# Asking for gathered edge tiles two at a time and announcing them two chunks later

## The chip, the cores and the metric

One core of a Trainium2 chip runs the whole program; the other cores are idle. The metric is the device time of one launch in microseconds, as a median over several launches. The engines are TensorE (PE), VectorE (DVE), ScalarE (ACT), GpSimd (POOL) and SyncE (SP); the last only starts transfers here, and POOL starts the indirect ones.

## The reference

50,000 nodes with 128 features, 50,000 edges sorted by target node. Two graph networks run one after the other. The first has three layers; `incidence[1]` is `dst`, so the messages are read at the targets and summed at `src`:

```python
for _ in range(DEPTH):                       # DEPTH = 3
    msgs = jnp.take(h, src, axis=0)
    msgs = jax.nn.relu(msgs @ W_edge + b_edge)
    agg = jax.ops.segment_sum(msgs, dst, num_segments=N_NODES)
    h = jax.nn.relu(jnp.concatenate([agg, h], axis=-1) @ W_agg + b_agg)
```

The second is a transformer layer on the same graph (queries, keys, values, edge features, a softmax over the edges of a node, a feed-forward part and layer norms). Both end in a residual sum and a layer norm.

## The kernel before, in words

The program is written by hand, stage by stage, with semaphores (`build`, line 1822):

- `sort_by_window` (line 193) sorts the edges by the 256-node block ("window", `W = 256`) in which their messages are summed, and makes the first messages. `window_tables` (line 535) computes tables from the sorted edges, among them `passed`: for each chunk of edge tiles, the number that the semaphore `tile_mm` must have reached once PE has used the chunk.
- `message_passing` (line 633) does the first two layers (`LAYERS - 1`), `last_layer` (line 925) the third one and the projections of the second network.
- `last_edges`, `attention` and `feed_forward` are the rest.

In the stages that the change touches, the messages of a layer lie in memory as rows of 3 x 128 bf16 numbers (`PARTS = 3`: high, middle and low part of a float). The sorted edges make 392 tiles of 128 edges (`NT`). For each tile POOL starts one indirect transfer, which gathers 128 rows of 768 bytes into one of 32 slots (`TILES`) of a ring in SBUF (`gathered`; line 759, in the last layer line 1076). PE multiplies each tile with a one-hot matrix made by DVE (`edge_hot`, line 856) and so sums the messages per node. It goes through 196 blocks of 256 nodes (`NW`), each with 3 tiles always (`ALWAYS`, of which neighbours share some), that is 9 matmuls on line 776, and rarely some more (`further`). After them come the product with the node's own row (line 794), and of the blocks before it the products for the next messages (lines 799 and 805). ACT and DVE close the block (lines 824 to 837, 874, 879), and SP stores it.

What POOL and PE tell each other:

- `g_in`: the transfers of a tile count up by 16 when they have landed.
- `tile_in`: POOL waits for `g_in` of a group of tiles and then adds their number (`tell`, lines 743 to 745 and 1060 to 1062). PE waits on it before a block: `pe.wait_ge(tile_in, layer * NT + first + ALWAYS)` (line 788).
- `tile_mm`: PE counts the blocks and extra tiles that it has added. Before POOL overwrites the slots of a chunk, it waits until `tile_mm` has reached the number in `passed` (lines 751 to 756). Those numbers are loaded to registers four at a time (lines 753 and 1070).

Before the change a chunk has 8 tiles (`CHUNK`), and tiles are announced in groups of 4 (`TOLD`). Within a chunk POOL issues eight gathers. The first group of the chunk is announced ahead of the eighth gather, the second group at the head of the next chunk, directly behind the gathers that it waits for:

```python
for c in range(NT // CHUNK):
    old = c - TILES // CHUNK
    if c:
        tell(c * CHUNK // TOLD - 1)      # waits for the 4 gathers issued last
```

All instructions of POOL are in one queue, in the order written.

Of the kernel before, what the change touches and what calls it, by code (L numbers as in the profile page):

```python
# [24 lines left out]
NT = NG * T  # L25
# [4 lines left out]
NW = NP // W  # L30
RING = 4
MSGS = 8
PARTS = 3
TILES = 32
CHUNK = 8
TOLD = 4
ALWAYS = 3
HOTS = 4
LAST = (N - (NG - 1) * GR) // T
# [1 line left out]
FAR = 65536  # L41
BIG = 3.0e38
EPS = 1e-5
assert NW % RING == 0 and NT % CHUNK == 0 and TILES % CHUNK == 0 and CHUNK % TOLD == 0
assert NG % 2 == 0 and (N - (NG - 1) * GR) % T == 0 and N == E


# [49 lines left out]
class Core:  # L97


    def __init__(self, nc, ctx):  # L100
# [23 lines left out]
        self.more_before = ctx.enter_context(nc.sbuf_tensor("more_before", [1, NW], I32))  # L124
        self.passed = ctx.enter_context(nc.sbuf_tensor("passed", [1, NT // CHUNK + 3], I32))
        self.column = ctx.enter_context(nc.sbuf_tensor("column", [P, 520], F32))
# [408 lines left out]
def window_tables(core):  # L535

    nc = core.nc
    with ExitStack() as s:
        def sb(nm, shape, dt):
            return s.enter_context(nc.sbuf_tensor("wt_" + nm, shape, dt))  # L540
        pair_i = sb("pair_i", [P, T, P, 2], I32)
        col_f, dst_f = sb("col_f", [P, T, P], F32), sb("dst_f", [P, T, P], F32)
        first_i, first_f, again, again_all = sb("first_i", [1, NT], I32), sb("first_f", [1, NT], F32), sb("again", [1, NT], F32), sb("again_all", [1, NT], F32)
        passed_f = sb("passed_f", [1, NT // CHUNK - 1], F32)
        filled, loaded, float_ok, transposed, tabs, chain = (core.sem("wt_" + x) for x in (
# [9 lines left out]
        def _(dve):  # L555
# [18 lines left out]
            dve.wait_ge(chain, 6)  # L574
            last = NT // CHUNK - 1
            chunks = [x[:, :].rearrange("a (c k) -> a c k", k=CHUNK) for x in (first_f, again_all)]
            nc.vector.scalar_tensor_tensor(out=passed_f[:, :], in0=chunks[0][:, 1:last + 1, 0], scalar=2.0, in1=chunks[1][:, 0:last, CHUNK - 1],
                                           op0=ALU.add, op1=ALU.add).then_inc(chain, 1)
# [54 lines left out]
def message_passing(core, W_edge, b_edge, W_agg, b_agg):  # L633
# [3 lines left out]
    with ExitStack() as s:  # L637
# [13 lines left out]
        wts, tabs_ok = core.sem("mp_weights_in"), core.sem("mp_place_tables")  # L651
        h_ld, h_st = ([core.sem(f"mp_{n}{r}") for r in range(RING)] for n in ("h_loaded", "h_stored"))
        m_st, m_uses = [core.sem(f"mp_m_stored{r}") for r in range(MSGS)], [(NW - r + MSGS - 1) // MSGS for r in range(MSGS)]
        g_in = [core.sem(f"mp_gathered{r}") for r in range(TILES // TOLD)]
        tile_in, edge_hot_ok, win_mm = core.sem("mp_tile_in"), core.sem("mp_edge_hots"), core.sem("mp_block_summed")
        more_hot_ok, tile_mm = ([core.sem(f"mp_{n}{layer}") for layer in range(LAYERS - 1)] for n in ("more_hots", "tiles_added"))
        h_ok, u_mm, u_ok, m_mm = core.sem("mp_h_ready"), core.sem("mp_u_product"), core.sem("mp_u_ready"), core.sem("mp_m_product")
# [35 lines left out]
        with nc.Block() as block:  # L693
# [41 lines left out]

            @block.gpsimd
            def _(pool):
                told = [0] * (TILES // TOLD)
                for layer in range(LAYERS - 1):
                    if layer:  # L740
                        for r in range(MSGS):
                            pool.wait_ge(m_st[r], 16 * layer * m_uses[r])
                    def tell(quarter):
                        pool.wait_ge(g_in[quarter % (TILES // TOLD)], 16 * TOLD * told[quarter % (TILES // TOLD)])
                        pool.sem_inc(tile_in, TOLD)

                    for c in range(NT // CHUNK):
                        old = c - TILES // CHUNK
                        if c:
                            tell(c * CHUNK // TOLD - 1)  # L750
                        if old >= 0:
                            if old % 4 == 0:
                                passed = nc.values_load_multi_w_load_instructions(
                                    core.passed[0:1, bass.ds(old, 4)], engines=[pool.engine], min_val=1, max_val=NW + NT + 1)[1]
                            pool.wait_ge(tile_mm[layer], passed[old % 4])
                            pool.nop(nofuse=True)
                        for i in range(c * CHUNK, (c + 1) * CHUNK):
                            r, q = i % TILES, i // TOLD % (TILES // TOLD)
                            pool.indirect_dma_start(gathered[:, r * PARTS * D:(r + 1) * PARTS * D], None, core.msg_rows[layer % 2],  # L759
                                                    bass.IndirectOffsetOnAxis(ap=core.other_idx[:, i:i + 1], axis=0)).then_inc(g_in[q], 16)  # L760
                            if i % TOLD == TOLD - 1:
                                if i % CHUNK >= TOLD:
                                    tell(i // TOLD - 1)
                                told[q] += 1
                    tell(NT // TOLD - 1)

            @block.tensor
            def _(pe):
# [156 lines left out]
def last_layer(core, W_agg, b_agg, x, w, b):  # L925
# [6 lines left out]
    with ExitStack() as s:  # L932
# [20 lines left out]
        wts, parts_c, zero_ok, tabs_ok = (core.sem("ll_" + n) for n in ("weights_in", "parts_chain", "zeros_ready", "place_tables"))  # L953
        h_ld, x_ld = [core.sem(f"ll_h_loaded{r}") for r in range(RING)], [core.sem(f"ll_x_loaded{q}") for q in range(Q)]
        st_x1, st = ([core.sem(f"ll_{n}{k}") for k in range(2)] for n in ("x1_stored", "proj_stored"))
        g_in = [core.sem(f"ll_gathered{r}") for r in range(TILES // TOLD)]
        tile_in, edge_hot_ok, block_mm, more_hot_ok, tile_mm = (core.sem("ll_" + n) for n in (
            "tile_in", "edge_hots", "block_summed", "more_hots", "tiles_added"))
        dst_hot_ok, dst_mm = core.sem("ll_dst_hots"), core.sem("ll_dst_counted")
# [95 lines left out]

        @block.gpsimd
        def _(pool):
            told = [0] * (TILES // TOLD)

            def tell(quarter):  # L1060
                pool.wait_ge(g_in[quarter % (TILES // TOLD)], 16 * TOLD * told[quarter % (TILES // TOLD)])
                pool.sem_inc(tile_in, TOLD)

            for c in range(NT // CHUNK):
                old = c - TILES // CHUNK
                if c:
                    tell(c * CHUNK // TOLD - 1)
                if old >= 0:
                    if old % 4 == 0:
                        passed = nc.values_load_multi_w_load_instructions(  # L1070
                            core.passed[0:1, bass.ds(old, 4)], engines=[pool.engine], min_val=1, max_val=NW + NT + 1)[1]
                    pool.wait_ge(tile_mm, passed[old % 4])
                    pool.nop(nofuse=True)
                for i in range(c * CHUNK, (c + 1) * CHUNK):
                    r, q = i % TILES, i // TOLD % (TILES // TOLD)
                    pool.indirect_dma_start(gathered[:, r * PARTS * D:(r + 1) * PARTS * D], None, core.msg_rows[(LAYERS - 1) % 2],  # L1076
                                            bass.IndirectOffsetOnAxis(ap=core.other_idx[:, i:i + 1], axis=0)).then_inc(g_in[q], 16)
                    if i % TOLD == TOLD - 1:
                        if i % CHUNK >= TOLD:
                            tell(i // TOLD - 1)  # L1080
                        told[q] += 1
            tell(NT // TOLD - 1)

        @block.tensor
        def _(pe):
# [736 lines left out]
def build(nc, a, out):  # L1822
    with ExitStack() as ctx:
        core = Core(nc, ctx)
        l1 = {name[7:]: ap for name, ap in a.items() if name.startswith("L1_gnn_")}
        make_identity(core)
        core.end_stage()
        sort_by_window(core, a["dst"], a["src"], a["x"], a["L0_gnn_W_edge"], a["L0_gnn_b_edge"], a["L0_gnn_W_agg"])
        core.end_stage()

        window_tables(core)
        core.end_stage()
        message_passing(core, a["L0_gnn_W_edge"], a["L0_gnn_b_edge"], a["L0_gnn_W_agg"], a["L0_gnn_b_agg"])
        core.end_stage()
        last_layer(core, a["L0_gnn_W_agg"], a["L0_gnn_b_agg"], a["x"], l1, l1)
        core.end_stage()
        last_edges(core)
        core.end_stage()
        attention(core, a["edge_attr_64"], l1["We"])
        core.end_stage()  # L1840
        feed_forward(core, l1, out)
# [16 lines left out]
```

## Time and profile before

| what | value |
|---|---|
| median of 3 launches | 5096.5 us (5095.79 to 5099.93) |
| profiled execution, span from first to last instruction | 6166.6 us |
| profiled execution, mean granted TensorE clock | 0.792 of full speed |
| busy over the span: PE, DVE, ACT, POOL | 74%, 59%, 34%, 51% |
| `sort_by_window` and `window_tables` | 0 to 857 us |
| `message_passing`, two layers | 858 to 2576 us |
| `last_layer` | 2576 to 3800 us |
| attention, then feed-forward | to 5150 us, to 6166 us |

The profiled execution's own time is its span: nothing else is printed for it. It is 1070 us longer than the median of the launches without a profile, and all durations below come from the profiled one. In the profile's rows PE's matmuls are pipelined, so their durations overlap; "issue" is idle time for which no releaser is seen.

### The profile page before, as it was taken

Reading aid. Unit: us, or ns where it says so; the run is one execution under the profiler, and the core shown is the slowest. Engines: PE = TensorE matmul, PEld = TensorE weight load, DVE = VectorE, ACT = ScalarE, POOL = GpSimd, SP = SyncE. Lnnn points to the kernel's source line nnn. Section 1 sums busy time; section 2 is a strip of 40 time slices with the busy share of each in tenths; the row PEclk is TensorE's granted clock in tenths of the full one; section 3 lists DMA queues with packets and bytes.
Section 4 is the critical chain, followed back from the end, with each engine's and each line's share of the span. In section 5 each row is a group of like instructions: output and inputs, shape, how many; then the busy total and the mean of one; then the engine's idle time right before and its main releaser. Section 6 shows DMA issues by size and latency. Waiting matters only on the chain. (4 is left out here: it accounts for less than half of the span.)

```text
span 6166.6 us, 106939 instructions
## 1 busy us (share of the span) xinstructions
PE 4568.4 (74%) x21995; PEld 2882.5 (47%) x21996; DVE 3657.1 (59%) x12075; ACT 2092.9 (34%) x4610; POOL 3168.2 (51%) x3348
## 2 busy tenths in 40 slices
PE   5666657777767777688888887566666666888887
PEld 3444435555555555555555554344444443333333
DVE  7666643333333333466666655677777776777777
ACT  0222223333333333322323323222222223666665
POOL 1555554444344444333333332666666664888887
PEclk9888878888888888889999998555555556999999
DMA  0333335555545555455665655333333332333333
GB/s 26 128 129 127 124 123 150 149 151 152 152 146 151 149 151 149 144 172 174 187 189 174 187 176 156 86 90 88 92 90 88 90 88 69 107 103 106 104 103 96
DMA packets 690049, 789.03 MB, mean 128 GB/s; under 512 B 145529, under 2 KB 545648, under 8 KB 689900
## 3 DMA queue, kind: packets, MB, share of 16 engines
q1 hardware_dynamic: 577004, 568.56, 28.9%
q0 software_dynamic: 112896, 218.94, 14.0%
q14 instruction: 112, 0.92, 0.1%
q8 instruction: 37, 0.61, 0.0%
HBM read 414.24 MB, written 372.92 MB: 128 GB/s over the span
## 5 line engine op out<-in xcount | busy, mean ns | idle before, releaser
L759 POOL DMA_INDIRECT mp_gathered<-msg_rows,other_idx x784 | 746.7, 952 | 947.8 <-PE bank L776 626.1
L776 PE MATMUL bank<-mp_edge_hot,mp_gathered 128*128 128x256 bf16 x3528 | 606.6, 304 | 279.3 <-issue 227.7
L1076 POOL DMA_INDIRECT ll_gathered<-msg_rows,other_idx x392 | 386.7, 987 | 782.8 <-PE bank L1096 607.7
L525 POOL DMA_INDIRECT by_window<-so_pay,so_pos_i x392 | 395.0, 1008 | 438.1 <-issue 303.9
L1363 POOL DMA_INDIRECT at_kv<-kv_rows,kv_idx x392 | 426.8, 1089 | 343.0 <-DVE at_v_e L1512 236.7
L776 PEld LDWEIGHTS bank<-mp_edge_hot,mp_gathered 128*128 x3528 | 373.4, 106 | 452.1 <-issue 383.9
L879 DVE TENSOR_TENSOR mp_msg_out<-mp_rest,mp_msg_out 128x256 bf16<-128x256 f32 x392 | 166.6, 425 | 649.1 <-ACT mp_msg_out L837 379.7
L1647 POOL DMA_INDIRECT ff_agg<-at_rows,last_idx x392 | 414.1, 1056 | 97.2 <-issue 89.7
L1365 POOL DMA_INDIRECT at_q<-q_rows,node_idx x392 | 390.0, 995 | 123.4 <-issue 123.4
L1143 PE MATMUL bank<-ll_weights,ll_x_cols 128*128 128x512 f32 x784 | 424.1, 643 | 4.5 <-issue 4.4
L824 ACT ACTIVATE mp_h_out<-bank,mp_b_agg 128x256 f32<-128x256 f32 x392 | 186.1, 475 | 702.3 <-PE bank L794 400.8
L1761 PE MATMUL bank<-ff_gelu,ff_w 128*128 128x512 f32 x784 | 412.9, 630 | 1.1 <-ACT ff_gelu L1793 1.1
L1753 PE MATMUL bank<-ff_h_cols,ff_w 128*128 128x512 f32 x784 | 386.7, 617 | 2.4 <-issue 2.4
L856 DVE TENSOR_SCALAR mp_edge_hot<-digits,mp_first_col,column 128x256 bf16<-128x256 bf16 x1176 | 336.9, 348 | 77.7 <-issue 48.9
L1096 PE MATMUL bank<-ll_gathered,ll_edge_hot 128*128 x3528 | 270.8, 226 | 141.4 <-issue 136.2
L794 PE MATMUL bank<-mp_h_in,mp_w_agg_h 128*128 128x256 f32 x784 | 305.0, 476 | 68.0 <-issue 65.2
L1424 PE MATMUL bank<-at_we,at_attr_cols 64*128 64x128 f32 x784 | 199.4, 431 | 193.2 <-ACT at_attr_cols L1458 100.3
L874 DVE TENSOR_TENSOR mp_rest<-bank,mp_msg_out 128x256 f32<-128x256 f32 x392 | 164.8, 420 | 294.8 <-issue 172.9
L406 DVE CUSTOM_DVE_ANT_0 so_picked<-so_onehot,bank 128x256 f32<-128x256 bf16 x392 | 164.4, 419 | 270.7 <-remote 158.8
L905 POOL TENSOR_TENSOR ff_rstd<-ff_eps_var,ff_half 128x4 f32<-128x4 f32 x294 | 307.1, 1045 | 24.5
L805 PEld LDWEIGHTS bank<-mp_w_agg_a,mp_msg_cols 128*128 128x128 f32 x1568 | 282.2, 228 | 77.2 <-issue 45.6
L805 PE MATMUL bank<-mp_w_agg_a,mp_msg_cols 128*128 128x128 f32 x1568 | 287.7, 314 | 29.1 <-issue 28.0
(247 smaller groups left out, 10008.7 us busy)
## 6 DMA issues: line engine op xcount, KB each, us to landing
msg_rows<-mp_msg_out SPq DMA_DIRECT2D x392, 192.0 KB
mp_h_in<-h_cols SPq DMA_DIRECT2D x392, 128.0 KB
h_cols<-mp_h_out SPq DMA_DIRECT2D x392, 128.0 KB
kv_rows<-ll_proj SPq DMA_DIRECT2D x98, 512.0 KB
msg_rows<-so_msg_out SPq DMA_DIRECT2D x98, 384.0 KB
h_cols<-so_h_out SPq DMA_DIRECT2D x98, 256.0 KB
ll_h_in<-h_cols SPq DMA_DIRECT2D x196, 128.0 KB
x_rows<-ll_x_b SPq DMA_DIRECT2D x98, 256.0 KB
```

The costliest lines, as they stand in the source:

```text
L525: pool.indirect_dma_start(core.by_window, bass.IndirectOffsetOnAxis(ap=pos_i[k][:, t:t + 1], axis=0), pay[k][:, t, :], None, bounds_check= ...
L759: pool.indirect_dma_start(gathered[:, r * PARTS * D:(r + 1) * PARTS * D], None, core.msg_rows[layer % 2], bass.IndirectOffsetOnAxis(ap=cor ...
L776: product = nc.tensor.matmul(agg_bank[k], gathered[:, bass.ds(at + d * D, D)], hot, start=(first and d == 0), stop=True, skip_group_check= ...
L805: product = nc.tensor.matmul(msg_bank[r % 2][:, c * P:(c + 1) * P], msg_c[r % 2][:, c * P:(c + 1) * P], w_agg_a[:, :], start=True, stop=True)
L856: return nc.vector.tensor_scalar(to, core.digits[:, :], first_col[:, bass.ds(n, 1)], core.column[:, bass.ds(i, 1)], ALU.add, ALU.is_equal)
L1076: pool.indirect_dma_start(gathered[:, r * PARTS * D:(r + 1) * PARTS * D], None, core.msg_rows[(LAYERS - 1) % 2], bass.IndirectOffsetOnAxis ...
L1143: nc.tensor.matmul(proj_bank[t][:, :], x1_cols[q % 2][:, t * P:(t + 1) * P], weights[:, :], start=t < T - BY_ACT, stop=True, skip_group_ch ...
L1363: pool.indirect_dma_start(kv[g % DEEP][:, t, :], None, core.kv_rows, bass.IndirectOffsetOnAxis(ap=core.kv_idx[:, at:at + 1], axis=0)).then ...
L1365: pool.indirect_dma_start(q[g % DEEP][:, t, :], None, core.q_rows, bass.IndirectOffsetOnAxis(ap=core.node_idx[:, at:at + 1], axis=0)).then ...
L1647: pool.indirect_dma_start(agg[g % 2][:, t, :], None, core.at_rows, bass.IndirectOffsetOnAxis(ap=core.last_idx[:, at:at + 1], axis=0)).then ...
L1753: nc.tensor.matmul(hid_bank[c][:, :], w1[:, c * P:(c + 1) * P], h_c[k][:, :], start=True, stop=True).then_inc(f1, 1)
L1761: product = nc.tensor.matmul(out_bank[k][:, :], w2[:, c, :], act_c[c][:, :], start=(c == 0), stop=(c == FC - 1))
```

## The change

`CHUNK` goes from 8 to 2. `TOLD` is gone: a chunk is also the group that is announced. It is announced after the gathers of the chunk two further on (`BEHIND = 2`), no longer directly behind its own. The wait for `tile_mm` and the two instructions around it come once for every 2 tiles, and the table `passed` has four times as many entries. There are 16 semaphores `g_in` in place of 8. The two stages are changed alike.

```diff
-CHUNK = 8
-TOLD = 4
+CHUNK = 2
+BEHIND = 2
@@ message_passing
-        g_in = [core.sem(f"mp_gathered{r}") for r in range(TILES // TOLD)]
+        g_in = [core.sem(f"mp_gathered{r}") for r in range(TILES // CHUNK)]
@@ pool
-                told = [0] * (TILES // TOLD)
                 for layer in range(LAYERS - 1):
+                    before = layer * NT // CHUNK
...
-                    def tell(quarter):
-                        pool.wait_ge(g_in[quarter % (TILES // TOLD)], 16 * TOLD * told[quarter % (TILES // TOLD)])
-                        pool.sem_inc(tile_in, TOLD)
+                    def tell(c):
+                        r = (before + c) % (TILES // CHUNK)
+                        pool.wait_ge(g_in[r], 16 * CHUNK * ((before + c) // (TILES // CHUNK) + 1))
+                        pool.sem_inc(tile_in, CHUNK)
 
                     for c in range(NT // CHUNK):
                         old = c - TILES // CHUNK
-                        if c:
-                            tell(c * CHUNK // TOLD - 1)
                         if old >= 0:
                             if old % 4 == 0:
                                 passed = nc.values_load_multi_w_load_instructions(
...
                         for i in range(c * CHUNK, (c + 1) * CHUNK):
-                            r, q = i % TILES, i // TOLD % (TILES // TOLD)
+                            r, q = i % TILES, (before + c) % (TILES // CHUNK)
                             pool.indirect_dma_start(gathered[:, r * PARTS * D:(r + 1) * PARTS * D], None, core.msg_rows[layer % 2],
                                                     bass.IndirectOffsetOnAxis(ap=core.other_idx[:, i:i + 1], axis=0)).then_inc(g_in[q], 16)
-                            if i % TOLD == TOLD - 1:
-                                if i % CHUNK >= TOLD:
-                                    tell(i // TOLD - 1)
-                                told[q] += 1
-                    tell(NT // TOLD - 1)
+                        if c >= BEHIND:
+                            tell(c - BEHIND)
+                    for c in range(NT // CHUNK - BEHIND, NT // CHUNK):
+                        tell(c)
```

POOL's queue in `message_passing` around the first time that slots are used again. "waits" lists the semaphores on which the instruction, or a bare wait just ahead of it, waits; where a semaphore number served an earlier stage, it stands here with that stage's name (the names with `so_` are those of `g_in`, and `so_ranks_ready` is `tile_mm`). Before:

```order
L759 DMA mp_gathered<-msg_rows,other_idx 128x384 [waits so_tables,so_flags]
L759 DMA mp_gathered<-msg_rows,other_idx 128x384 x7
L753 TENSOR_LOAD passed [waits so_flags_stored,so_onehots]
L753 ISA x8
L759 DMA mp_gathered<-msg_rows,other_idx 128x384 [waits so_ranks_ready]
L759 DMA mp_gathered<-msg_rows,other_idx 128x384 x7
L759 DMA mp_gathered<-msg_rows,other_idx 128x384 [waits so_bits,so_columns,so_ranks_ready]
L759 DMA mp_gathered<-msg_rows,other_idx 128x384 x7
```

After (here `mp_tiles_added0` is `tile_mm`):

```order
L753 TENSOR_LOAD passed [waits so_ranks_ready]
L753 ISA x8
L759 DMA mp_gathered<-msg_rows,other_idx 128x384 [waits mp_tiles_added0]
L759 DMA mp_gathered<-msg_rows,other_idx 128x384
L759 DMA mp_gathered<-msg_rows,other_idx 128x384 [waits so_ranks_read,mp_tiles_added0]
L759 DMA mp_gathered<-msg_rows,other_idx 128x384
L759 DMA mp_gathered<-msg_rows,other_idx 128x384 [waits so_positions,mp_tiles_added0]
L759 DMA mp_gathered<-msg_rows,other_idx 128x384
L759 DMA mp_gathered<-msg_rows,other_idx 128x384 [waits so_bits,mp_tiles_added0]
L759 DMA mp_gathered<-msg_rows,other_idx 128x384
L753 TENSOR_LOAD passed [waits so_columns]
L753 ISA x8
```

The waits for landings and for PE move from every eighth gather to every second one, and a load of four table entries with its eight register instructions comes before every eighth gather, not before every thirty-second. PE's queue has the same instructions as before.

## Rows read from the trace of the kernel before

**Rows 1.** The page's first line.

```profile
span 6166.6 us, 106939 instructions
```

**Rows 2.** Stretches: PE, PEld, DVE, ACT, POOL busy (instructions); granted clock; DMA share; GB/s

```profile
858.00:1712.00 854.00, 637.48 (x3359) 472.80 (x3359) 307.36 (x988) 297.47 (x783) 373.20 (x392) 0.83 0.50 150
1712.00:2576.00 864.00, 633.00 (x3359) 473.54 (x3359) 312.98 (x991) 299.12 (x785) 373.51 (x392) 0.82 0.50 150
2576.00:3800.00 1224.00, 1032.15 (x6621) 649.99 (x6621) 777.79 (x3066) 355.58 (x785) 386.71 (x392) 0.91 0.59 179
```

**Rows 3.** Waits of PE, 858 to 2576 us: total us, times, longest.

```profile
PE bank L776 <- issue: 263.0, 335, 4.4
PE bank L776 <- POOLq L745: 52.1, 13, 14.0
```

**Rows 4.** Waits of POOL, same stretch.

```profile
POOL mp_gathered L759 <- PE bank L776: 626.1, 85, 10.0
POOL mp_gathered L759 <- DMA mp_gathered<-msg_rows,other_idx: 26.6, 18, 3.2
```

**Rows 5.** PE's register instructions on L776: ns min/median/max, first and last start.

```profile
L776 PEldq FUSED_REGOPS  x3600: 2/46/1399, 866.0 to 2567.9; - x190
```

**Rows 6.** PE's timeline (start, us): two starts of a block, then a stall within a block.

```profile
1309.46 1.15 PE L776 MATMUL bank<-mp_edge_hot,mp_gathered 128*128 128x256 bf16 x9
...
1311.76 1.15 PE L776 MATMUL bank<-mp_edge_hot,mp_gathered 128*128 128x256 bf16 x9
...
1317.75 0.41 PE L776 MATMUL bank<-mp_edge_hot,mp_gathered 128*128 128x256 bf16 x2 [1.28 <-issue]
```

**Rows 7.** PE's timeline: two starts of a block at half clock.

```profile
1670.38 2.13 PE L776 MATMUL bank<-mp_edge_hot,mp_gathered 128*128 128x256 bf16 x9
...
1674.86 1.22 PE L776 MATMUL bank<-mp_edge_hot,mp_gathered 128*128 128x256 bf16 x9
```

**Rows 8.** POOL's timeline (start, us): seventh and eighth gather of the first chunk, later chunk heads.

```profile
865.85 0.95 POOL L759 DMA_INDIRECT mp_gathered<-msg_rows,other_idx  x1 [0.30 <-issue]
867.10 0.95 POOL L759 DMA_INDIRECT mp_gathered<-msg_rows,other_idx  x1 [0.30 <-issue]
870.57 0.95 POOL L759 DMA_INDIRECT mp_gathered<-msg_rows,other_idx  x1 [2.52 <-DMA mp_gathered<-msg_rows,other_idx]
...
882.84 0.95 POOL L759 DMA_INDIRECT mp_gathered<-msg_rows,other_idx  x1 [2.57 <-DMA mp_gathered<-msg_rows,other_idx]
...
895.56 0.95 POOL L759 DMA_INDIRECT mp_gathered<-msg_rows,other_idx  x1 [2.99 <-DMA mp_gathered<-msg_rows,other_idx]
...
909.49 1.01 POOL L759 DMA_INDIRECT mp_gathered<-msg_rows,other_idx  x1 [4.14 <-PE bank L776]
```

**Rows 9.** POOL's queue: the load of L753, the wait instruction of L756.

```profile
L753 POOLq TENSOR_LOAD <-passed x24: 322/326/545, 907.2 to 2512.6; - x24
...
L756 POOLq EVENT_SEMAPHORE  x90: 17/17/17, 908.7 to 2519.9; - x90
```

**Rows 10.** Instructions that mark the groups of the sort, last layer and attention.

```profile
L525 POOL DMA_INDIRECT by_window<-so_pay,so_pos_i x392: 969/974/1245, 128.1 to 834.9; - x196
...
L1143 PE MATMUL bank<-ll_weights,ll_x_cols x784: 589/592/1221, 2648.6 to 3796.8; 128*128 128x512 f32 x196
...
L1363 POOL DMA_INDIRECT at_kv<-kv_rows,kv_idx x392: 943/949/1860, 3812.9 to 5093.8; - x196
```

**Rows 11.** Timelines of POOL and ACT: two group starts each, sort, last layer, attention.

```profile
141.74 1.09 POOL L525 DMA_INDIRECT by_window<-so_pay,so_pos_i  x1 [3.45 <-issue]
...
147.00 1.10 POOL L525 DMA_INDIRECT by_window<-so_pay,so_pos_i  x1 [0.33 <-issue]
...
2773.96 0.60 ACT L1173 ACTIVATE ll_x_cols<-bank 128x512 f32<-128x512 f32 x1 [7.93 <-PE bank L1132]
...
2783.36 0.60 ACT L1173 ACTIVATE ll_x_cols<-bank 128x512 f32<-128x512 f32 x1 [2.92 <-PE bank L1132]
...
4314.32 0.95 POOL L1363 DMA_INDIRECT at_kv<-kv_rows,kv_idx  x1 [4.36 <-DVE at_v_e L1512]
...
4325.43 0.95 POOL L1363 DMA_INDIRECT at_kv<-kv_rows,kv_idx  x1 [0.30 <-issue]
```

**Rows 12.** Waits of POOL in the last layer, 2576 to 3800 us.

```profile
POOL ll_gathered L1076 <- PE bank L1096: 607.7, 43, 20.6
```

More of the change, by code:

```diff
@@ L43 @@
 EPS = 1e-5
-assert NW % RING == 0 and NT % CHUNK == 0 and TILES % CHUNK == 0 and CHUNK % TOLD == 0
+assert NW % RING == 0 and NT % CHUNK == 0 and TILES % CHUNK == 0 and ALWAYS + BEHIND * CHUNK < TILES - 2 * CHUNK
 assert NG % 2 == 0 and (N - (NG - 1) * GR) % T == 0 and N == E
@@ L955, in last_layer @@
         st_x1, st = ([core.sem(f"ll_{n}{k}") for k in range(2)] for n in ("x1_stored", "proj_stored"))
-        g_in = [core.sem(f"ll_gathered{r}") for r in range(TILES // TOLD)]
+        g_in = [core.sem(f"ll_gathered{r}") for r in range(TILES // CHUNK)]
         tile_in, edge_hot_ok, block_mm, more_hot_ok, tile_mm = (core.sem("ll_" + n) for n in (
@@ L1057, in _, with tell @@
         def _(pool):
[L1058 to L1062, printed above, removed]
+            def tell(c):
+                pool.wait_ge(g_in[c % (TILES // CHUNK)], 16 * CHUNK * (c // (TILES // CHUNK) + 1))
+                pool.sem_inc(tile_in, CHUNK)
             for c in range(NT // CHUNK):
                 old = c - TILES // CHUNK
-                if c:
-                    tell(c * CHUNK // TOLD - 1)
                 if old >= 0:
@@ L1074, in _ @@
                 for i in range(c * CHUNK, (c + 1) * CHUNK):
-                    r, q = i % TILES, i // TOLD % (TILES // TOLD)
+                    r, q = i % TILES, c % (TILES // CHUNK)
                     pool.indirect_dma_start(gathered[:, r * PARTS * D:(r + 1) * PARTS * D], None, core.msg_rows[(LAYERS - 1) % 2],
                                             bass.IndirectOffsetOnAxis(ap=core.other_idx[:, i:i + 1], axis=0)).then_inc(g_in[q], 16)
[L1078 to L1082, printed above, removed]
+                if c >= BEHIND:
+                    tell(c - BEHIND)
+            for c in range(NT // CHUNK - BEHIND, NT // CHUNK):
+                tell(c)
         @block.tensor
```

## Prediction

> **What bounds the kernel now.** I read the stretches first, then each engine's waits, then timelines. The two layers of message passing take 854 and 864 us of the profiled span [rows 2]. PE looks like the bound there: POOL spends 626.1 us waiting for PE to free slots, PE only 52.1 us waiting for POOL to announce tiles [rows 3, 4]. Taken at its word this says that nothing POOL does matters. But the span is 6166.6 us [rows 1] against a median of 5096.5 us without the profiler, and PE's idle time is mostly "issue", 263.0 us on the edge matmuls alone [rows 3]. It falls between matmuls of one block, where no semaphore is waited for [rows 6]. There even register instructions of PE, which touch nothing outside their queue, take 46 ns at the median and up to 1399 [rows 5]. I read that as PE's queue held up by the recording of its own many instructions, which is absent in a launch that is timed. POOL has few instructions, and its gathers come at a steady beat. So each engine must be priced without the stalls.
>
> PE: undisturbed, a block starts every 1311.76 - 1309.46 = 2.30 us [rows 6]; at half clock every 1674.86 - 1670.38 = 4.48 us [rows 7]. Two layers have 392 blocks: 902 us at full clock.
>
> POOL: two gathers are 1.25 us apart within a chunk (867.10 - 865.85). Where POOL does not wait for PE, the next chunk's first gather starts 3.47 us after the eighth (870.57 - 867.10), because the announcement waits for the gather just issued to land. The chunk heads are 12.27 and 12.72 us apart (882.84 - 870.57, 895.56 - 882.84) [rows 8]. I take 7 x 1.25 + 3.5 = 12.25 us for 8 tiles. Two layers have 98 chunks: 1201 us, and 24 loads of table entries in the same queue. The first load starts at 907.2, the wait instruction behind it at 908.7, with 545 ns in the load itself; at the median of 326 ns that is 1.3 us [rows 9]. 24 x 1.3 = 31, so POOL needs **1232 us** where PE needs 902. Without recording, POOL's queue bounds this stage: 3.14 us per block.
>
> A ledger checks this. The 1070 us between profile and median must come from stages with stalls. Sort: groups run from 128.1 to 834.9 us, 707 us for 98, while an undisturbed one takes 5.26 us, so 515: 192 us gone. Last layer: 1148 us from first to last projection against 98 x 9.40 = 921: 227. Attention: 1281 against 98 x 11.11 = 1089: 192 [rows 10, 11]. That leaves 1070 - 611 = 459 us for message passing: 1718 - 459 = 1259 us. POOL's bound with some 25 us at the layers' heads and ends gives 1257. With PE the bound at full clock it would be about 930, and the ledger would be 330 us off. The ledger is rough (one group stands for 98), but it sides with POOL.
>
> **The change part by part.**
> *Landing waits gone.* An announcement now waits for tiles whose last gather started 4 gathers, 5.0 us, earlier, and they have landed by then: the 3.47 us of the boundary hold landing and the start of the next gather both. Each boundary of eight gives up 3.5 - 1.25 = 2.25 us. There are 96 in two layers (the announcement that ends a layer stays): **-216 us**. Bounds: 2.2 (870.57) to 2.7 us (895.56) [rows 8], so -211 to -259.
> The boundary is also priced by a rule. The Trainium skill ("DMA: Bandwidth & Descriptors", Anatomy of one DMA) gives a transfer from GpSimd 2.0 us plus bytes over 436e3; for 98,304 bytes an estimate of 2.23 us. With the 0.8 us to the next gather the boundary would be 3.0 us, not 3.47, and the whole sum 48 us smaller in gain. The trace decides, for 3.47.
>
> *Waits every second gather.* Per pair POOL now issues one announcement and one wait for `tile_mm`, 17 ns each [rows 9]. Once a wait is over, a gather starts 909.49 - 908.7 = 0.8 us later [rows 8, 9]. An announcement already stands ahead of every eighth gather, and that gather still starts 1.25 us after the seventh with 0.30 us idle [rows 8]: the queue runs ahead, beneath the 0.95 us of the gather that executes. With 0.3 us until the queue is free, 0.1 for two instructions and 0.8 for the start there are 1.2 of 1.25 us used. I take **0**. Lower bound 0, since nothing is removed here. Upper bound 0.6 us per pair: the wait holds until the gather ahead is done, 0.95 + 0.1 + 0.8 = 1.85 in place of 1.25, so 0.6; times 392 pairs that is 235 us. I lean to the low end since the row of the eighth gather is this very case.
>
> *Loads.* 180 chunks of a layer wait for slots, with a load for every fourth: 45, before 12. Two layers: 90 for 24. A load in a running burst costs 0.3 + 0.1 + 1.3 + 0.8 - 1.25 = 1.2 us: 90 x 1.2 = 108, less the 31 of before: **+77 us**. Bounds: 0.7 us each if part of it is hidden (+32), 1.5 with the longest load seen (+104).
>
> *First announcement.* PE's first block needs 3 tiles. Before, tiles 0 to 3 are announced ahead of the eighth gather; now tiles 2 and 3 behind it: 1.3 us later in each of three layers. It costs only where PE then sets the pace, **+2 us** with the last layer's.
>
> *Last layer.* POOL waits 607.7 us for PE there [rows 12] of 1224, and needs 49 x 12.25 = 600 us where an undisturbed stage takes 921. Its queue stays hidden; with 343 fewer waits it could be faster without anyone seeing it. The cover is PE's and DVE's work of 9.40 us per group against POOL's 6.1. **0 us.** The longer `passed` table costs DVE a fraction of a microsecond.
>
> Sum: -216 + 77 + 2 = -137 us. POOL's queue falls to 784 x 1.25 + 108 = 1088 us, 2.78 us per block, still above PE's 2.30, so PE's full-clock pace does not cut the gain. The sum is made on differences in the profiled execution's durations and applied to the median, as the recording stalls that separate the two are on PE and not in these terms: 5096.5 - 137 = **4960 us**.
>
> **The rivals.**
> *A. PE bounds the stage in timed launches too.* Granted clock in message passing is 0.82 to 0.83 [rows 2]; at 4.48 us a block for part of the time PE could average 3.1 to 3.3 us, and the ledger's 1259 us (3.2 per block) fits that as well. The waits of rows 3 and 4 then tell the truth. Against it: the clock is lower where PE is less busy (0.83 with PE busy 75% of the stretch, 0.91 with 84% [rows 2]), and without stalls and without waits for POOL nothing would leave PE idle to keep it down. Then the change moves POOL's slack alone: 5096.5 + 2, range 5080 to 5100. A mixture (PE the bound in half of the time) gives about 5028 and belongs to my range.
> *B. The wait breaks POOL's run-ahead.* Asking before every second gather ties POOL to each gather's end: 235 us more, and loads as before. -216 + 77 + 235 = +96: about 5193 if POOL is the bound. It decides from (216 - 77) / 392 = 0.35 us per pair; below that the change still gains. For it: only 0.05 us of slack in my count. Against it: the eighth gather.
> *C. The transfers become the bound.* DMA share is 0.50 at 150 GB/s [rows 2]; squeezed to 1120 us it would be 0.77. Landing times then grow; up to 5.0 us they stay hidden. If half of the gain is lost so, 5028.
>
> **How the numbers follow.** Forecast with its sizes somewhat off: 0.65. A: 0.16. B: 0.12, of which a third is too mild to be slower than noise. C or the mixture: 0.07. Low end: -259 + 32 = -227, little of it likely together: 4890. The high end takes in C and most of A's neighbourhood: 5092. Changes within 0.2% (10 us, about what a measurement of this kernel can tell from none) are same. Faster 0.74: forecast, C, and a part of A and B. Same 0.15: most of A. Slower 0.11.
>
> **What would show it.** In the changed profile POOL's waits on its own landings (26.6 us in 18 pieces [rows 4]) are gone; where POOL runs free, pairs follow each other at 1.25 us, with one 2.4 us step every 8 gathers; at 1.8 us or more per pair head B holds. In the profile itself the stage shrinks little, since PE's stalls remain: 1718 us to between 1640 and 1720, and POOL's long waits for PE turn into many short ones. If the time is within 10 us of before, A is right and my reading of the stalls is wrong.

## The result and the profile after

The changed kernel takes **4900.4 us** (median of 4, 4899.9 to 4902.8) against 5097.4 us before (median of 4, 5095.8 to 5099.9): a ratio of 0.9616, 95% interval 0.9604 to 0.9627, 197 us or 3.8% faster. The forecast was 4960, range 4890 to 5092.

```profile
span 4898.1 us, 108529 instructions
```

This span is within 2 us of the execution's own time, and it records as many instructions of PE as before. In some periods a chip runs the kernel before in 5974 to 6199 us: by its span and stalls the first profile [rows 1, 5] falls in one, and so do the runs with BEHIND = 0, BEHIND = 1 and chunks of 4, each compared with the kernel before run beside it.

The kernel before was profiled again (the run "before again"). Its page begins, and PE's register instructions on L776 read:

```profile
span 5081.5 us, 106939 instructions
...
L776 PEldq FUSED_REGOPS  x3600: 46/46/65, 679.4 to 1978.0; - x190
```

As many instructions are recorded as in [rows 1] and [rows 5], and the longest of these takes 65 ns, not 1399. So the 1070 us between the first profile and the median are not the price of recording.

The stretches that answer to [rows 2], of before again (first layer, second, last; columns as there):

```profile
672.00:1329.00 657.00, 555.48 (x3359) 436.71 (x3359) 308.77 (x997) 291.23 (x784) 375.77 (x392) 0.92 0.65 197
1329.00:1989.00 660.00, 554.90 (x3359) 433.61 (x3359) 305.42 (x985) 290.74 (x784) 376.19 (x393) 0.93 0.64 195
1989.00:2959.00 970.00, 923.55 (x6627) 576.69 (x6627) 780.28 (x3076) 356.05 (x785) 386.67 (x395) 0.98 0.75 226
```

and of the changed kernel:

```profile
672.00:1233.00 561.00, 510.26 (x3359) 413.54 (x3359) 306.60 (x998) 288.49 (x784) 376.75 (x393) 0.98 0.77 231
1233.00:1799.00 566.00, 515.82 (x3359) 416.83 (x3359) 302.77 (x981) 288.83 (x784) 376.75 (x392) 0.97 0.76 227
1799.00:2768.00 969.00, 921.85 (x6627) 575.48 (x6627) 781.68 (x3079) 355.94 (x785) 375.09 (x395) 0.98 0.73 227
```

Message passing falls from 1317 to 1127 us. The last layer takes 970 and 969 us: nothing. PE is busy 84% of the stretch before and 91% after, and its granted clock goes from 0.92 and 0.93 to 0.98 and 0.97. The transfers' share goes from 0.65 to 0.77.

The waits of POOL and PE that answer to [rows 3, 4], of before again from 670 to 1990 us:

```profile
POOL mp_gathered L759 <- DMA mp_gathered<-msg_rows,other_idx: 168.9, 82, 3.7
POOL mp_gathered L759 <- PE bank L776: 83.3, 23, 5.5
POOL ll_gathered L1076 <- POOLq L144: 20.9, 1, 20.9
POOL mp_gathered L759 <- DMA msg_rows<-mp_msg_out: 19.2, 1, 19.2
...
PE bank L776 <- POOLq L745: 150.1, 66, 13.4
```

and of the changed kernel, from 670 to 1800 us:

```profile
POOL ll_gathered L1071 <- POOLq L144: 51.4, 1, 51.4
POOL mp_gathered L759 <- DMA msg_rows<-mp_msg_out: 49.9, 1, 49.9
POOL mp_gathered L759 <- PE bank L775: 42.8, 58, 3.2
...
POOL mp_gathered L759 <- DMA mp_gathered<-msg_rows,other_idx: 20.1, 66, 0.3
...
PE bank L775 <- POOLq L747: 52.2, 26, 14.3
```

Here, without PE's stalls, POOL waited for its own landings, 169 us, where [rows 4] had 27, and PE waited for POOL. That is what the prediction inferred for a launch without stalls. After the change the landing waits are gone (no piece is longer than 0.3 us, the gap that stands between any two gathers), and the two waits between a layer's last gather and the next one's first (20.9 and 19.2 us) have grown to 51.4 and 49.9: PE now ends a layer later than POOL.

POOL's timeline of before again (start, duration): the eighth gather of a chunk and the head of the next, once where a load of table entries stands between and once without.

```profile
718.22 0.98 POOL L759 DMA_INDIRECT mp_gathered<-msg_rows,other_idx  x1 [0.30 <-issue]
724.53 0.95 POOL L759 DMA_INDIRECT mp_gathered<-msg_rows,other_idx  x1 [5.33 <-issue]
...
733.35 0.95 POOL L759 DMA_INDIRECT mp_gathered<-msg_rows,other_idx  x1 [0.30 <-issue]
736.83 0.94 POOL L759 DMA_INDIRECT mp_gathered<-msg_rows,other_idx  x1 [2.54 <-DMA mp_gathered<-msg_rows,other_idx]
```

The head without a load comes 3.48 us after the gather before it, as in [rows 8]; the one with a load 6.31. Over both layers the 72 heads without a load average 3.70 us, the 24 with one 5.42. Together that is 396 us, where 96 steps of 1.25 would be 120: 276 us of POOL's queue.

The same timeline of the changed kernel, over a stretch in which a load is executed:

```profile
762.29 0.99 POOL L759 DMA_INDIRECT mp_gathered<-msg_rows,other_idx  x1 [0.30 <-PE bank L775]
763.59 0.95 POOL L759 DMA_INDIRECT mp_gathered<-msg_rows,other_idx  x1 [0.30 <-issue]
764.84 0.95 POOL L759 DMA_INDIRECT mp_gathered<-msg_rows,other_idx  x1 [0.30 <-PE bank L775]
766.09 1.00 POOL L759 DMA_INDIRECT mp_gathered<-msg_rows,other_idx  x1 [0.30 <-issue]
767.39 0.94 POOL L759 DMA_INDIRECT mp_gathered<-msg_rows,other_idx  x1 [0.30 <-issue]
```

Every gather follows the one before at 1.25 to 1.30 us; the load starts at 763.1. The trace holds 90 loads:

```profile
L753 POOLq TENSOR_LOAD <-passed x90: 322/341/1145, 711.9 to 1734.5; - x90
```

The 90 gathers behind a load start 1.44 us after the one before on average, 74 of them less than 1.6 us, so all loads together cost the queue at most 17 us.

The ledger from first gathers: layer one's gathers 636.8 to 509.5 us, layer two's 637.5 to 514.2, so 251 us less; the turn of POOL to layer two 20.2 to 50.9 and to the last layer 21.9 to 52.4 us, 61 us given back. 251 - 61 = 190 us. The two spans differ by 183, as the rest of the program came out some 6 us longer in this pair. In the run with the change in message passing alone, on the same chip as before again, the span is 191 us shorter, 190 of them in this stage.

What paces PE now is seen in its timeline in the changed kernel: ordinary blocks, and one in which it loads the table of the next eight blocks.

```profile
1001.88 0.70 PE L793 MATMUL bank<-mp_h_in,mp_w_agg_h 128*128 128x256 f32 x2
...
1004.44 0.69 PE L793 MATMUL bank<-mp_h_in,mp_w_agg_h 128*128 128x256 f32 x2
...
1006.92 0.70 PE L793 MATMUL bank<-mp_h_in,mp_w_agg_h 128*128 128x256 f32 x2
```

```profile
942.81 0.70 PE L793 MATMUL bank<-mp_h_in,mp_w_agg_h 128*128 128x256 f32 x2
...
945.17 1.70 PE L775 MATMUL bank<-mp_edge_hot,mp_gathered 128*128 128x256 bf16 x9 [0.78 <-DVE mp_edge_hot L855]
947.07 0.69 PE L793 MATMUL bank<-mp_h_in,mp_w_agg_h 128*128 128x256 f32 x2 [0.21 <-issue]
```

```profile
L680 PEldq TENSOR_LOAD <-spans x50: 592/776/1262, 675.7 to 1778.3; - x50
...
L680 PEldq TENSOR_LOAD <-spans x1: 1040/1040/1040, 943.5 to 943.5; - x1
```

Ordinary blocks are 2.56 and 2.48 us apart, the one with the load (line 680) 4.26. The second row is the load of that block: it holds PE's queue until 944.5, just before the late edge matmuls, so the 0.78 us that the view puts down to DVE are the load's. The mean over a layer is 2.78 and 2.81 us, of which 0.13 at most are waits for POOL (52 us in all): PE, not POOL at 2.50, sets the pace.

### The profile page after: what moved, and what is told of

It is laid out like the page before. It is cut to its first block and busy times, and to the rows that moved or that the text cites. A ratio compares the mean times of both kernels' runs of the same rounds, so it can differ in the third digit from the quotient of the medians.

```text
span 4898.1 us, 108529 instructions
## 1 busy us (share of the span) xinstructions
PE 4105.9 (84%) x21995; PEld 2654.1 (54%) x21996; DVE 3644.4 (74%) x12075; ACT 2076.8 (42%) x4610; POOL 3180.5 (65%) x3348
## 5 line engine op out<-in xcount | busy, mean ns | idle before, releaser
L775 PE MATMUL bank<-mp_edge_hot,mp_gathered 128*128 128x256 bf16 x3528 | 476.5, 275 | 61.8 <-POOLq L747 34.9
L1359 POOL DMA_INDIRECT at_q<-q_rows,node_idx x392 | 410.6, 1047 | 119.4 <-issue 119.4
L775 PEld LDWEIGHTS bank<-mp_edge_hot,mp_gathered 128*128 x3528 | 346.5, 98 | 133.8 <-issue 91.0
L1137 PE MATMUL bank<-ll_weights,ll_x_cols 128*128 128x512 f32 x784 | 405.1, 619 | 0.0
L1793 ACT ACTIVATE ff_xhat<-ff_y,ff_shift,ff_rstd 128x128 f32<-128x128 f32 x392 | 161.6, 482 | 333.9 <-DVE ff_shift L1669 332.1
L793 PE MATMUL bank<-mp_h_in,mp_w_agg_h 128*128 128x256 f32 x784 | 275.0, 433 | 11.0 <-issue 9.0
L1787 ACT ACTIVATE ff_gelu<-bank,ff_bf 128x512 f32<-128x512 f32 x392 | 245.4, 675 | 58.1 <-PE bank L1747 58.1
L1747 PEld LDWEIGHTS bank<-ff_h_cols,ff_w 128*128 128x128 f32 x784 | 154.4, 197 | 199.2 <-issue 171.9
L804 PEld LDWEIGHTS bank<-mp_w_agg_a,mp_msg_cols 128*128 128x128 f32 x1568 | 238.3, 192 | 21.9 <-ACT mp_msg_cols L827 1.2
L1707 DVE SCALAR_TENSOR_TENSOR ff_v<-ff_deviation,ff_rstd,ff_x 128x128 f32<-128x128 f32 x392 | 114.6, 352 | 173.6 <-POOL ff_rstd L904 171.8
```

The source lines that it names most:

```text
L775: product = nc.tensor.matmul(agg_bank[k], gathered[:, bass.ds(at + d * D, D)], hot, start=(first and d == 0), stop=True, skip_group_check= ...
L1137: nc.tensor.matmul(proj_bank[t][:, :], x1_cols[q % 2][:, t * P:(t + 1) * P], weights[:, :], start=t < T - BY_ACT, stop=True, skip_group_ch ...
L1359: pool.indirect_dma_start(q[g % DEEP][:, t, :], None, core.q_rows, bass.IndirectOffsetOnAxis(ap=core.node_idx[:, at:at + 1], axis=0)).then ...
L1747: nc.tensor.matmul(hid_bank[c][:, :], w1[:, c * P:(c + 1) * P], h_c[k][:, :], start=True, stop=True).then_inc(f1, 1)
```

## The experiments

**Before again** (no edit).

> The kernel before, unchanged, for a second profile. Theory 1 (the first profile of the kernel before was of an execution that was itself 1070 us longer, and its PE stalls are no part of a normal one): span within 10 us of 5097, no gaps of over 1 us between the nine edge matmuls of a block, message passing 1258 to 1330 us with chunk heads of POOL 12.2 to 12.7 us apart and POOL waiting for PE under 60 us. Rival (PE bounds message passing in every launch): span near 5097 too, but POOL waits for PE over 150 us in message passing. It also tells how long the last layer takes: the changed kernel has it at 978 us; under theory 1 within 10 us of that, under theory 2 (the finer asking helped the last layer) 1020 to 1050 us.

Span 5081.5 us, time 5083.3. Theory 1 holds in its main points: stage 1317 us, PE's waits for POOL 150 us. Chunk heads without a load are 12.2 to 13.7 us apart, 12.5 at the median, so some exceed the 12.7 expected. POOL's waits for PE, 83 us, lie between the two theories' numbers. The last layer takes 970 us, so theory 2 falls.

**Half of the change each.** In the first, the last layer keeps chunks of 8 and a second table for them; in the second, message passing does.

```diff
+CHUNK8 = 8
+TOLD = 4
...
-for c in range(NT // CHUNK):
+for c in range(NT // CHUNK8):      # shortened: in one stage only
```

> Message passing as changed, the last layer with chunks of 8 and announcements of 4. Theory 1 (all of the gain is in message passing): 4900, within 10 us of the changed kernel. Theory 2 (the last layer gave what the prediction missed, 60 us): 4950 to 4965, and the last layer's stretch longer by that.

> The last layer as changed, message passing with chunks of 8 and announcements of 4. Theory 1: 5097, within 10 us. Theory 2: 5035 to 5050. The sum of this run's gain and that of the other half should be 197 us if the two stages are independent.

Message passing alone: 4894.4 us against 5085.4, ratio 0.9626 (0.9610 to 0.9642). Last layer alone: 5085.1, ratio 0.9998 (0.9989 to 1.0008). All of the gain is in message passing; the last layer's cover held, as forecast.

**Landing wait alone.** Chunks stay at 8; the second announcement of a chunk moves behind the fourth gather of the next one.

```diff
-                        if c:
-                            tell(c * CHUNK // TOLD - 1)
...
-                                if i % CHUNK >= TOLD:
+                                if i >= TOLD:
                                     tell(i // TOLD - 1)
```

> The kernel before with one thing changed in both stages: the second group of 4 of a chunk is announced behind the fourth gather of the next chunk, not at its head. Chunks stay at 8, table loads as before. It takes away the landing wait alone. Theory 1 (landing wait is what is paid): message passing shrinks by 96 x 2.25 = 216 us less the waits for PE that come back; 4890 to 4930 in all if the last layer does not matter. Theory 3 (the coarse asking costs too, since 8 slots are asked for at once and the ring runs full): only 90 to 150 us gained, 4950 to 5005, and POOL waits for PE in pieces of some us at the chunk heads.

4899.5 us against 5085.4, ratio 0.9631 (0.9615 to 0.9647): all but 5 us of what message passing alone gives on the same chip (4894.4), with one announcement moved. Its stretches of message passing, beside 561 and 566 us of the changed kernel:

```profile
673.00:1236.00 563.00, 513.43 (x3359) 416.98 (x3359) 306.35 (x998) 289.31 (x784) 379.50 (x393) 0.98 0.76 230
1236.00:1805.00 569.00, 515.45 (x3359) 415.72 (x3359) 300.73 (x982) 288.99 (x784) 378.93 (x392) 0.98 0.74 226
```

So the chunk size has a part of 5 us at most in this result. Theory 3 falls.

**Four times the loads.** The changed kernel, with a load of four entries, each from the entry that the pair needs, ahead of every pair.

```diff
-                            if old % 4 == 0:
+                            if True:
...
-                            pool.wait_ge(tile_mm[layer], passed[old % 4])
+                            pool.wait_ge(tile_mm[layer], passed[0])
```

> The changed kernel with a load of four table entries ahead of every second gather, not of every eighth: 270 loads more in message passing. Theory 1 (POOL's queue runs ahead of the gathers that execute, so a load costs nothing while it fits beneath two gathers, 2.5 us): within 15 us of the changed kernel. The prediction's price (1.2 us each, exposed): 320 us more in message passing alone. Between (the queue needs 0.3 to 0.5 us beyond two gathers for each pair): 100 to 200 us more, less what PE's slower pace hides.

4980.5 us against 5098.0, ratio 0.9770 (0.9754 to 0.9786). That is 80 us slower than the changed kernel, below the 100 to 200 of the nearer of the two dear prices. POOL's timeline, then the loads ahead of the third and of the fifth of these gathers, and all of them:

```profile
902.99 0.99 POOL L759 DMA_INDIRECT mp_gathered<-msg_rows,other_idx  x1 [1.02 <-PE bank L775]
904.28 1.04 POOL L759 DMA_INDIRECT mp_gathered<-msg_rows,other_idx  x1 [0.30 <-issue]
906.00 0.95 POOL L759 DMA_INDIRECT mp_gathered<-msg_rows,other_idx  x1 [0.68 <-issue]
907.26 0.95 POOL L759 DMA_INDIRECT mp_gathered<-msg_rows,other_idx  x1 [0.31 <-issue]
908.51 0.94 POOL L759 DMA_INDIRECT mp_gathered<-msg_rows,other_idx  x1 [0.30 <-PE bank L775]
...
L753 POOLq TENSOR_LOAD <-passed x1: 953/953/953, 903.3 to 903.3; - x1
...
L753 POOLq TENSOR_LOAD <-passed x1: 326/326/326, 906.4 to 906.4; - x1
...
L753 POOLq TENSOR_LOAD <-passed x360: 321/956/2054, 708.8 to 1859.4; - x180
```

A pair starts 3.01 us (906.00 - 902.99) after the last where its load takes 953 ns, and 2.51 us where it takes 326. So this edit changed two things, the number of the loads and their length. The 90 loads that start at an entry whose number is a multiple of four, as all loads of the changed kernel do, take 0.36 us on average, and the gather behind them starts 1.31 us after the one before. The other 270 take 1.11 us, and the step is 1.91. Why the first entry matters the runs don't show. The layers' gathers grow by 82 and 69 us, and the turns at their ends shrink back from 51 and 52 to 18 and 20, so 85 us in the stage. The cost is that of the long loads: a short one is hidden even directly behind a pair whose load was long. Short loads ahead of every pair were not run.

**Load ahead of the landing wait.** The kernel before, with the load of the next entries moved above the announcement at the chunk head.

```diff
+                        if old >= 0 and old % 4 == 0:
+                            passed = nc.values_load_multi_w_load_instructions(
+                                core.passed[0:1, bass.ds(old, 4)], engines=[pool.engine], min_val=1, max_val=NW + NT + 1)[1]
                         if c:
                             tell(c * CHUNK // TOLD - 1)
                         if old >= 0:
-                            if old % 4 == 0:
-                                passed = nc.values_load_multi_w_load_instructions(
...
```

> The kernel before, with the load of table entries put ahead of the announcement at the chunk head, so that it runs while the landing is waited for. In the second profile of the kernel before, chunk heads without a load are 3.4 to 3.6 us behind the gather before, those with one 5.3 to 6.1. If that difference is the load standing behind the landing wait: 24 x 1.3 to 2.1 = 30 to 50 us less, 5035 to 5055. If it is something else that comes every fourth chunk (PE's wait for slots): within 10 us of before.

5071.1 us against 5098.0, ratio 0.9945 (0.9929 to 0.9962): 27 us, just below the range. The heads with a load average 4.10 us, down from 5.42 in before again, so the load did stand behind the landing wait, at 1.3 us each: 24 x 1.3 = 31. But the 72 heads without one rise from 3.70 to 3.96, 19 us, so some 12 us are left in the stage. The kernel before was not profiled on this chip, and where the other 15 us of the 27 lie stays open.

**Less work for PE.** In both kernels `add_tile` of message passing leaves out the third part of each message (the low parts are missing from the sums).

```diff
-                        for d in range(PARTS):
+                        for d in range(PARTS - 1):
```

> The changed kernel; in message passing PE adds two of the three parts of each message, 6 edge matmuls per block instead of 9, so the low parts are missing from the sums. Theory 4 (after the change PE bounds message passing: its lag behind POOL grows to the full ring and takes 30 us more at each layer's end): its stage falls by 60 to 100 us to POOL's 1.25 us per gather, 4800 to 4840. Rival (POOL is the bound after the change as the prediction said): within 15 us of 4900.

> The kernel before with the same matmuls left out. Theory 1 (POOL's queue bounds message passing before the change): 5097 less at most 20 us (the 83 us that POOL waits for PE in 23 pieces can give back a part), so 5060 to 5097. Rival A of the prediction (PE is the bound before the change too): 5000 or less.

The changed kernel: 4820.1 us, 80 us below its 4900. Its stretches and the turns at the layers' ends:

```profile
673.00:1202.00 529.00, 457.56 (x2762) 359.41 (x2762) 306.74 (x999) 289.15 (x784) 380.14 (x393) 0.98 0.81 245
1202.00:1726.00 524.00, 455.02 (x2762) 360.44 (x2762) 302.48 (x983) 289.25 (x784) 376.37 (x393) 0.97 0.81 245
```

```profile
POOL ll_gathered L1071 <- POOLq L144: 20.2, 1, 20.2
```

The kernel before: 5086.2 us against 5098.0, ratio 0.9976 (0.9967 to 0.9986), 12 us. The same cut in PE's work is worth 80 us after the change and 12 before. POOL bounded the stage before; PE bounds it after. Rival A and the prediction's own statement that PE would not cut the gain both fall. So does rival C: the stage got shorter with the transfers' share at 0.81 and 245 GB/s, above the 0.77 of the changed kernel.

**No distance between gather and announcement.** `BEHIND = 0`, otherwise as changed; the kernel before took 5998 us beside it.

> The changed kernel with BEHIND = 0: each pair of tiles is announced directly behind its own gathers. This puts a landing wait behind every second gather, four times as many as before the change. Theory 1 (a landing wait costs POOL 2.2 us and POOL then bounds): a pair takes 1.25 + 3.5 = 4.75 us, message passing 392 x 4.75 = 1862 us plus 90 loads of 1.3 to 2.1: 5700 to 5850 in all, the last layer (196 x 4.75 = 931 plus loads, against PE's 920) longer by 20 to 120 us as well. If small chunks were good in themselves, less than 5400.

6419.5 us in one run, against 5998.1: 421 us slower, where the changed kernel is faster. POOL's timeline shows the wait behind each pair:

```profile
1002.07 0.96 POOL L759 DMA_INDIRECT mp_gathered<-msg_rows,other_idx  x1 [0.31 <-issue]
1007.02 0.95 POOL L759 DMA_INDIRECT mp_gathered<-msg_rows,other_idx  x1 [3.99 <-PE bank L775]
1008.27 0.94 POOL L759 DMA_INDIRECT mp_gathered<-msg_rows,other_idx  x1 [0.30 <-issue]
1012.26 0.99 POOL L759 DMA_INDIRECT mp_gathered<-msg_rows,other_idx  x1 [3.04 <-DMA mp_gathered<-msg_rows,other_idx]
```

The heads come 4.95 and 3.99 us after the gather before, 1.5 and 0.5 more than the 3.5 expected. The absolute time can't be compared with the expectation, which was written for a kernel before of 5097 us; direction and place are as expected. Small chunks are worth nothing without the distance.

**Distance of one chunk, with chunks of 2 and of 4.**

```diff
-CHUNK = 2
-BEHIND = 2
+CHUNK = 2        # in the other run: 4
+BEHIND = 1
```

> The changed kernel with BEHIND = 1: an announcement waits for tiles whose last gather started two gathers (2.5 us) earlier. Landings take 2.7 us from the start of the gather. Theory 1: the queue is held up to 2.7 us and loses its run-ahead: each pair 2.7 + 0.1 + 0.8 = 3.6 us after the last gather it waits for, which is 2 x 1.25 = 2.5 plus 1.1, so a pace of about 3.6 us per pair at worst; message passing up to 1400 us, 5000 to 5180 in all. If the queue's start time of 0.8 us is hidden all the same: within 40 us of the changed kernel.

> The changed kernel with chunks of 4 and BEHIND = 1: an announcement waits for tiles whose last gather started four gathers (5.0 us) earlier, as in the changed kernel, with half of its waits, announcements and loads. Theory 1 (only the age of the landing that is waited for counts): within 10 us of the changed kernel. If the number of waits costs something: 10 to 60 us less than the changed kernel.

> The kernel with BEHIND = 1 again, since its first run fell on a chip where the kernel before takes 5998 us, not 5097, and the changed kernel has no time there. On a chip where the kernel before takes 5080 to 5100: if the landing waited for is too young (2.7 us from the start of the gather against 2.5 us until the next start), 5000 or more; if POOL's start time is hidden beneath the gather that executes and PE's pace bounds all the same, 4895 to 4925. On a slow chip: near 5483, a ratio near 0.915.

All three fell where the kernel before takes 5998 or 6181 us. Chunks of 2: 5482.7 us against 5998.1, ratio 0.9148 (0.9118 to 0.9179), and again 5662.2 against 6181.3, ratio 0.9151 (0.9122 to 0.9180), the ratio expected for such a chip, though not the time. Chunks of 4: 5549.0, ratio 0.9236 (0.9201 to 0.9271). The gain is larger there, 8.5% with chunks of 2, and chunks of 4 lose 66 us to chunks of 2, though the landings they wait for are older; nothing here explains either. The numbers expected beside 5080 to 5100 us were not tested, and the changed kernel itself has no time beside these.

The stalls of [rows 5] are there too. In the second of these runs, chunks of 2 again:

```profile
L775 PEldq FUSED_REGOPS  x3600: 2/46/737, 865.7 to 2289.3; - x190
```

## Why the prediction was right in direction and short in size

- **What bounds.** Right: without PE's stalls POOL's queue bounds message passing, at 3.3 us per block against 3.14 worked out. The run with less work for PE before the change gives 12 us and shows it. Wrong: the cause of the stalls. I read them as the price of recording; before again records as many instructions of the same kernel without them, and the changed kernel's trace as many of PE's. What held PE's queue up in the first profile stays open. It was luck that the forecast came to no harm by this: the launches of the result had no such stalls, but not for the reason given.
- **The ledger** gave the stage 1259 us, POOL's pace 1257; it takes 1317. The undisturbed groups of the sort and attention were good (first to last gather of the sort 520 us against 515); the last layer took 970 us, not the 921 plus 75 of heads and ends that its group and stretch gave, so the ledger was off by stages as well.
- **Landing waits, -216 us.** Right in mechanism, undersized: the heads without a load average 3.70 us, not 3.5, so 96 x (3.70 - 1.25) = 235. By the Trainium skill's figure ("DMA: Bandwidth & Descriptors", Anatomy of one DMA), from which the prediction worked out an estimate of 3.0 us for the boundary, the term would have been further off.
- **Waits every second gather, 0.** Right in number; rival B did not happen. Heads of pairs without a load start 1.31 us after the gather before, and 1.26 in the run with less work for PE. But the evidence was misread, and in so far it was luck. No announcement stands ahead of the eighth gather, other than the section on the kernel before and the prediction say: `tell` (line 763) comes behind the gather of its turn in the loop, and the order of the queue shows seven gathers without a wait behind each chunk's head. Both groups of a chunk are announced behind its eighth gather. What the first profile does show is this row:

```profile
L745 POOLq EVENT_SEMAPHORE  x1: 17/17/17, 865.9 to 865.9; - x1
```

The queue was through with the announcement behind the eighth gather at 865.9, and that gather started at 867.10 [rows 8]: the queue runs about one gather ahead of the engine. The +2 us for the first announcement rested on the same misreading: tiles 2 and 3 are announced behind the eighth gather before and after.
- **Loads, +77 us.** This is the term that failed. Before the change a load cost 5.42 - 3.70 = 1.7 us behind the landing wait, 24 x 1.7 = 41 us, and all of that went; after it the 90 loads cost at most 17 us, which the sum below counts among other waits. -41 and at most +17 stand in place of +77: some 100 us. I had charged a load in full behind the gather in front of it. The queue takes it up before that gather starts (load at 763.1, gather at 763.59, in the timeline above), so a load of 0.3 to 0.4 us is through in time. The run with four times the loads shows a limit: loads of 1.1 us are not.
- **PE's pace does not cut the gain.** Wrong, and it hid the error above; that the time lies in the range owes something to this. PE needs about 2.7 us per block, not 2.30: one block in eight carries a load of its own and takes 4.3 on average, and the others take 2.5 to 2.7. It then falls behind POOL by the whole ring and gives back 61 us at the layers' ends.
- **The sum.** -235 - 41 = -276 of POOL's queue, then 61 given back at the ends and about 25 of other waits inside the layers, the loads' 17 among them: -190 in the stage, against -137 forecast.
- **Last layer, 0.** Right, 0.9998.

## What to carry to other kernels

An engine whose queue both starts transfers and announces them should wait for a landing only after several further starts: here a wait for a transfer just started cost 2.45 us each, and moving one announcement gave 3.7%. Before a wait or a load in a queue is priced, look at how far the queue runs ahead of its engine, and at how long each load takes. Here it was free while it fitted beneath the gathers that executed meanwhile, and beyond that only the excess showed. And read in the kernel, not from the times of a trace, in which order a queue stands: an instruction of the queue can be over before the transfer ahead of it starts. And when one engine's queue is relieved, take the next engine's mean pace, with its rare long blocks, and not the pace of a good stretch.

## What the runs showed of the hardware

- POOL's queue hid a load of four table entries (341 ns at the median, 1.3 us with its register instructions) beneath indirect gathers of 0.95 us each: the gather behind it started 1.44 us after the one before on average, against 1.31 at pairs without a load.
- The same load from an entry whose number is not a multiple of four took 1.11 us on average instead of 0.36 (270 and 90 loads of one run), and the gather behind it started 1.91 us after the one before instead of 1.31.
- PE's granted clock rose from 0.92 and 0.93 to 0.98 and 0.97 in the two layers of message passing when its waits for POOL fell, without any change to PE's own instructions.
- PE's register instructions, at most 65 ns long in an execution of 5081 us, took up to 1399 in one of 6167 us of the same kernel. The cause was not found. A profile whose span is far above the median of the launches should be taken again before it is argued from.
